# 64 wide attention of a fused transformer kernel: scores two heads at a time, turning two pairs behind, reciprocals of sums by pair

## What is computed

```python
def _L2_xattn_ref(x, context, w_q, w_k, w_v, w_o, b_o):
    HEADS = 16
    DIM_HEAD = 64
    SCALE = DIM_HEAD ** (-0.5)
    q = (x @ w_q).reshape(B, Sq, HEADS, DIM_HEAD).transpose(0, 2, 1, 3)
    k = (context @ w_k).reshape(B, Skv, HEADS, DIM_HEAD).transpose(0, 2, 1, 3)
    v = (context @ w_v).reshape(B, Skv, HEADS, DIM_HEAD).transpose(0, 2, 1, 3)
    sim = jnp.einsum('bhid,bhjd->bhij', q, k) * SCALE
    attn = jax.nn.softmax(sim, axis=-1)
    out = jnp.einsum('bhij,bhjd->bhid', attn, v)
    return out.transpose(0, 2, 1, 3).reshape(B, Sq, INNER) @ w_o + b_o
x = x + jnp.tanh(g_xattn[2]) * _L2_xattn_ref(_layernorm(x), ctx_768, ...)
```

## Time and profile before

| | |
|---|---|
| median of 3 runs | 2455.58 us |
| the profiled execution: its time, its span | 2458.67 us, 2456.9 us |
| PE matmul busy over the span | 1932.6 us (79%) |
| DVE, ACT, POOL busy | 1015.9, 732.9, 999.5 us |
| stage l2x, from its first scores to the last gathered copy | 990.9 to 1573.4 us |
| PE at L1900, L1913, L1928: share of the span on the chain that ended last | 5%, 3%, 3% |

### The profile page before, as it was taken

The page is one execution under the profiler, slowest core; times in us unless marked ns, Lnnn a source line. Parts: engine busy times, 40 slices in busy tenths (PEclk is TensorE's granted clock), DMA queues, the critical chain, the costliest instruction groups (busy, mean ns, idle before and its releaser), DMA issues.

```text
span 2456.9 us, 33526 instructions
## 1 busy us (share of the span) xinstructions
PE 1932.6 (79%) x11738; PEld 1465.6 (60%) x11738; DVE 1015.9 (41%) x2339; ACT 732.9 (30%) x1721; POOL 999.5 (41%) x1044
## 2 busy tenths in 40 slices
PE   3589599727999962898988989769981899647997
PEld 2477466426888852555655656569970666435664
DVE  2434478531222212433334323543223578443773
ACT  1122056302222210332333323312330355312564
POOL 4010443064666643432344323461666676303320
PEclk9799789558999985888988989879995689766999
DMA  4270446114565543000000000012752645004441
GB/s 141 96 259 0 61 75 99 56 65 149 186 200 187 199 149 124 4 3 3 3 0 3 3 3 0 1 54 65 248 165 68 88 67 76 2 0 67 77 72 40
DMA packets 123393, 194.15 MB, mean 79 GB/s; under 512 B 12128, under 2 KB 99168, under 8 KB 122560
## 3 DMA queue, kind: packets, MB, share of 16 engines
q1 hardware_dynamic: 94288, 144.84, 24.6%
q0 software_dynamic: 8480, 26.65, 3.4%
q10 hardware_dynamic: 20496, 20.97, 2.6%
HBM read 109.84 MB, written 43.52 MB: 62 GB/s over the span
## 4 chain that ended last, share of the span: by engine, by line
PE 61%; issue 15%; POOL 9%; DVE 8%; DMA 3%; SPq 2%; ACT 2%; DVEq 0%; POOLq 0%; ACTq 0%
PE bank L2264 8%; PE bank L1774 6%; PE bank L2051 5%; PE bank L1900 5%; PE bank L1775 5%; PE bank L1776 5%; PE bank L1877 5%; PE bank L2085 3%; PE bank L1913 3%; PE bank L1928 3%; POOL arena L853 2%; PE bank L1890 2%; DVE nmf L1133 2%; SPq L582 1%; POOL rows_by_expert L835 1%
## 5 line engine op out<-in xcount | busy, mean ns | idle before, releaser
L1133 DVE TENSOR_REDUCE nmf<-bank 128x2 f32<-128x512 f32 x384 | 257.4, 688 | 144.8 <-PE bank L2051 142.9
L1625 ACT ACTIVATE pT<-bank 128x512 f32<-128x512 f32 x384 | 225.5, 595 | 224.2 <-PE bank L2065 222.7
L1774 PE MATMUL bank<-split,ewl 128*128 128x256 f32 x818 | 245.3, 300 | 9.6 <-DVE split L1361 9.6
L1371 DVE TENSOR_TENSOR arena<-sil,bank 128x256 f32<-128x256 f32 x216 | 91.1, 422 | 358.9 <-ACT sil L1709 358.8
L1776 PE MATMUL bank<-split,ewh 128*128 128x256 f32 x818 | 233.2, 285 | 0.0
L1775 PE MATMUL bank<-split,ewh 128*128 128x256 f32 x818 | 233.1, 285 | 0.0
L2051 PE MATMUL bank<-kpack,qpack 48*128 48x256 f32 (+1 forms) x768 | 199.6, 361 | 33.1 <-DVE nmf L1133 18.9
L889 POOL TENSOR_TENSOR esum<-esum,minus 128x2 f32<-128x2 f32 x128 | 89.2, 697 | 324.4 <-ACT arena L1555 324.2
L1489 ACT ACTIVATE arena<-bank 128x512 f32<-128x512 f32 x162 | 96.7, 597 | 388.4 <-PE bank L2264 158.5
L2264 PE MATMUL bank<-ew,arena 128*128 128x256 f32 (+1 forms) x864 | 210.2, 389 | 2.1 <-issue 2.1
L823 POOL TENSOR_TENSOR ewl<-ew,ewh 128x1536 fp32r<-128x1536 f32 (+1 forms) x71 | 206.9, 2914 | 5.7
(11 more groups left out here) (403 smaller groups left out, 3844.1 us busy)
## 6 DMA issues: line engine op xcount, KB each, us to landing
ew<-in_we SPq DMA_DIRECT2D x46, 768.0 KB, 4.5
rows_by_expert<-mrow ACTq DMA_DIRECT2D x1, 20480.0 KB, 62.8
qpack<-qhl SPq DMA_DIRECT2D x144, 128.0 KB
kpack<-khl SPq DMA_DIRECT2D x144, 128.0 KB
ew<-in_we SPq DMA_DIRECT2D x23, 640.0 KB, 5.5
ew<-in_we SPq DMA_DIRECT2D x25, 512.0 KB, 4.4
arena<-rows_by_expert SPq DMA_DIRECT2D x46, 256.0 KB, 3.8
rows_by_expert<-arena SPq DMA_DIRECT2D x46, 256.0 KB, 4.1
```

Source lines behind the costliest of these rows:

```text
L1133: V.tensor_reduce(nmf[:, c, :, j, r], bank[h % 2][:, :].rearrange("p (t k) -> p t k", t=T), AXX, ALU.max, negate=True).then_inc(m["mx"], 1)
L1625: A(pT16[i % 8][:, :], bank[2 + h % 2][:, :], ACT.Exp, scale=s.qscale).then_inc(m["e"], 1)
L1774: mm(out_, al, bh, start=start, stop=False)
```

## The change

- PE's scores come by pair p (heads 2p and 2p + 1). The four matmuls alternate: queries 0 to 127 of the even head, of the odd head, then queries 128 to 255 of both. The pair waits for the exponentials of head 2p - 2 (its second bank is that head's).
- PE's `heads` goes over pairs: scores of pair p, turn_probs of both heads of pair p - 2, values of pair p - 3. At p = 4 the turning of xn stands between the turns and the values.
- DVE goes over pairs too: both maxima, then both copies of pair p - 2. The statistics of batch n + 1 come behind the copies of p = 2, xn behind those of p = 4. In batch 7 the statistics for the next stage come once per pair.
- POOL takes the sums of a pair to the power -1 in one 128 x 4 operation, then makes the two products. The root comes behind pair 0, that is behind two products in place of one.
- ACT has the same exponentials and gathered copies, by pair.
- prob has 5 buffers in place of 3, and probT 6 in place of 8, in the same room.

```diff
@@ -357,8 +356,8 @@
         qT = q8
         kT = cut(8 * S).rearrange("p (g s) -> p g s", g=8)
         v = cut(T * NH * 64).rearrange("p (t n) -> p t n", t=T)
-        prob = [cut(512) for _ in range(3)]
-        probT = [cut(512) for _ in range(8)]
+        prob = [cut(512) for _ in range(5)]
+        probT = [cut(512) for _ in range(6)]
         oTs = cut(8 * S).rearrange("p (g s) -> p g s", g=8)
         on = [sb(f"on{t}", [P, D]) for t in range(T)]
         xt2 = arena[:, ARENA - DC * S:ARENA].rearrange("p (c s) -> p c s", c=DC)
@@ -883,16 +882,18 @@
                     m = ph[name]
 
                     def normalise(n, ahead):
-                        for h in range(NH):
-                            pool.wait_ge(m["e"], n * NH + h + 1)
-                            nc.gpsimd.tensor_tensor(esum[:, h, :], esum[:, h, :], minus1[:, 0:T], ALU.pow)\
+                        for p in range(PAIRS):
+                            pool.wait_ge(m["e"], n * NH + 2 * p + 2)
+                            sums = esum[:, 2 * p:2 * p + 2, :]
+                            nc.gpsimd.tensor_tensor(sums, sums, minus1[:, :].rearrange("p (h t) -> p h t", t=T), ALU.pow)\
                                 .then_inc(m["psum"], 1)
-                            pool.wait_ge(m["psum"], n * NH + h + 1)
-                            p3 = prob[h % 3].rearrange("p (t k) -> p t k", t=T)
-                            nc.gpsimd.tensor_tensor(p3, p3, esum[:, h, :].rearrange("p (t o) -> p t o", o=1)
-                                                    .broadcast_to([P, T, S]), ALU.mult).then_inc(m["pn"], 1)
-                            if h == 0 and ahead:
+                            pool.wait_ge(m["psum"], n * PAIRS + p + 1)
+                            for h in (2 * p, 2 * p + 1):
+                                p3 = prob[h % 5].rearrange("p (t k) -> p t k", t=T)
+                                nc.gpsimd.tensor_tensor(p3, p3, esum[:, h, :].rearrange("p (t o) -> p t o", o=1)
+                                                        .broadcast_to([P, T, S]), ALU.mult).then_inc(m["pn"], 1)
+                            if p == 0 and ahead:
                                 root(m, n + 2, rstd[:, :], rstd[:, :], mhalf[:, 0:T])
 
                     root(m, 1, rstd[:, :], rstd[:, :], mhalf[:, 0:T])
@@ -1044,27 +1045,30 @@
                         src = bank[s.jobs[j]][:, :].rearrange("p (k s) -> p k s", k=2)
                         ts(qT[:, 2 * j:2 * j + 2, :], src, s.qscale, None, ALU.mult).then_inc(m["qc"], 1)
 
-                def heads(n, ahead, steps_=None):
-                    for h in steps_ or range(LAG, NH + LAG):
-                        if h < NH:
-                            dve.wait_ge(m["s"], n * NH + h + 1)
-                            V.tensor_reduce(nmax[:, h, :], bank[h % 3][:, :].rearrange("p (t k) -> p t k", t=T),
-                                            AXX, ALU.max, negate=True).then_inc(m["mx"], 1)
-                        if h >= LAG:
-                            k = h - LAG
-                            dve.wait_ge(m["pT"], n * NH + k + 1)
-                            if k >= 8:
-                                dve.wait_ge(m["pv"], n * s.groups + (k - 8) // s.per + 1)
-                            V.tensor_copy(probT[k % 8][:, :], bank[3 + k % 2][:, :]).then_inc(m["pTc"], 1)
-                        if h == LAG and ahead:
+                def maximum(n, h):
+                    dve.wait_ge(m["s"], n * NH + h + 1)
+                    V.tensor_reduce(nmax[:, h, :], bank[h % 3][:, :].rearrange("p (t k) -> p t k", t=T),
+                                    AXX, ALU.max, negate=True).then_inc(m["mx"], 1)
+                def turned_weights(n, k):
+                    dve.wait_ge(m["pT"], n * NH + k + 1)
+                    if k >= 6:
+                        dve.wait_ge(m["pv"], n * s.groups + (k - 6) // s.per + 1)
+                    V.tensor_copy(probT[k % 6][:, :], bank[3 + k % 2][:, :]).then_inc(m["pTc"], 1)
+                def heads(n, ahead):
+                    for p in range(1, PAIRS + 2):
+                        for h in (2 * p, 2 * p + 1):
+                            if p < PAIRS:
+                                maximum(n, h)
+                        for h in (2 * p, 2 * p + 1):
+                            if p >= 2:
+                                turned_weights(n, h - 4)
+                        if p == 2 and ahead:
                             statistics(n + 1)
-                        if isinstance(n, int) and n == B - 1 and 0 <= h - 4 < B - 1 and not steps_:
-                            stats_of(h - 4)
-                        if h == FRONT and ahead:
+                        if isinstance(n, int) and n == B - 1 and 2 <= p < 2 + (B - 1):
+                            stats_of(p - 2)
+                        if p == 4 and ahead:
                             front(n + 1)
 
                 def finish(n):
...
                         .then_inc(m["oc"], 1)
 
-                def heads(n, steps_=None):
-                    nf = 0
-                    for h in steps_ or range(LAG, NH + LAG + 2):
-                        if h < NH:
-                            act.wait_ge(m["mx"], n * NH + h + 1)
-                            if h >= 3:
-                                act.wait_ge(m["pT"], n * NH + h - 2)
-                            for t in range(T):
-                                ins = A(prob[h % 3][:, t * S:(t + 1) * S], bank[h % 3][:, t * S:(t + 1) * S], ACT.Exp,
-                                        bias=nmax[:, h, t:t + 1], accum_out=esum[:, h, t:t + 1])
-                            ins.then_inc(m["e"], 1)
-                        if h == FRONT + 1 and not isinstance(n, int):
+                def exponent(n, h):
+                    act.wait_ge(m["mx"], n * NH + h + 1)
+                    if h >= 5:
+                        act.wait_ge(m["pT"], n * NH + h - 4)
+                    for t in range(T):
+                        ins = A(prob[h % 5][:, t * S:(t + 1) * S], bank[h % 3][:, t * S:(t + 1) * S], ACT.Exp,
+                                bias=nmax[:, h, t:t + 1], accum_out=esum[:, h, t:t + 1])
+                    ins.then_inc(m["e"], 1)
+                def heads(n):
...
+                            if p < PAIRS:
+                                exponent(n, h)
+                        if p == 5 and not isinstance(n, int):
                             front(n + 1)
-                        if nf < s.fills and h == min((nf + 1) * 2 * s.per - 1 + LAG + 2, NH + LAG + 1):
-                            gathered(n, nf)
-                            nf += 1
-                    assert steps_ or nf == s.fills
+                        if p >= 5 and p % 2 == 1:
+                            gathered(n, (p - 5) // 2)
 
                 front(0)
                 projected(0)
-                heads(0, range(LAG))
+                for h in range(2):
+                    exponent(0, h)
                 with act.Fori(0, B - 1) as n:
                     heads(n)
                     projected(n + 1)
-                    heads(n + 1, range(LAG))
+                    for h in range(2):
+                        exponent(n + 1, h)
                 heads(B - 1)
 
             def packing(s):
@@ -1891,15 +1899,17 @@
                                      start=c == 0, stop=c == s.kt - 1)
                         ins.then_inc(m["v"], 1)
 
-                def scores(n, h):
-                    if h >= 3:
-                        pe.wait_ge(m["e"], n * NH + h - 2)
-                    gr = h // s.per
-                    r0 = 64 * (h % s.per)
-                    for t in range(T):
-                        ins = mm(bank[h % 3][:, t * S:(t + 1) * S], qT[r0:r0 + 64, gr, t * P:(t + 1) * P],
-                                 kT[r0:r0 + 64, gr, :], start=True, stop=True)
-                    ins.then_inc(m["s"], 1)
+                def scores(n, p):
+                    if p >= 1:
+                        pe.wait_ge(m["e"], n * NH + 2 * p - 1)
+                    for t in range(T):
+                        for j in range(2):
...
@@ -1934,22 +1944,19 @@
                     pe.wait_ge(m["qc"], (n + 1) * s.qjobs)
                     pe.wait_ge(m["kc"], (n + 1) * s.qjobs)
                     pe.wait_ge(m["vc"], (n + 1) * s.vjobs)
-                    for h in range(LAG):
-                        scores(n, h)
+                    scores(n, 0)
 
                 def heads(n, ahead):
-                    gr = 0
-                    for h in range(LAG, NH + LAG + 1):
-                        if h < NH:
-                            scores(n, h)
-                        if h < NH + LAG:
-                            turn_probs(n, h - LAG)
-                        if h == FRONT + 1 and ahead:
+                    for p in range(1, PAIRS + 3):
+                        if p < PAIRS:
+                            scores(n, p)
+                        if 0 <= p - 2 < PAIRS:
+                            turn_probs(n, 2 * p - 4)
```

(53 more changed lines are left out.)

## The result

| | before | changed |
|---|---|---|
| median | 2455.19 us (4 runs, 2451.28 to 2457.07) | 2397.62 us (4 runs, 2389.51 to 2402.51) |
| ratio | | 0.9764, 95% interval 0.9732 to 0.9796 |
| profiled execution, span | 2458.67, 2456.9 us | 2394.44, 2392.6 us |
| stage l2x, first scores to the last finish | 582.59 us | 531.88 us |
| all the rest of the span | 1874.3 us | 1860.7 us |

The median fell by 57.6 us, against 58 predicted. The stage itself fell by 50.7, though; the rest of the span, whose instructions are the same, was 13.6 shorter in this trace. In the changed kernel's second trace, on one of these, the stage is 531.97 and the rest 1895.6. So I compare the length of the stage, and the ratio to the kernel before on the same chip.

What follows compares the result with a forecast made beforehand. PE alone was taken to bound the heads at full clock, POOL's root their start. Batches 1 to 6 give -45.1, batch 0 -5, batch 7 -6, batch 5's projection -2: together -58 from 2455.6, 2398 us, range 2380 to 2430.

Steps and rivals of the forecast that it cites:

- A pair at full clock, 3.15: Heads, PE: scores 1.11, turns 1.03 and values 1.01 make 3.15 us a pair against 4.31.
- The start of the heads: From finish's last issue: a new 3.5 us wait on PE, the wait on the root 5 us later, then one for xn.
- The walk: Step-by-step timing of a looped batch's heads from finish's last issue: 40.7 us against 48.0 with the clock as before.
- the new wait for xn: PE turns xn at 22.3 instead of 20.9, behind DVE's maxima and copies; cost 1.5 us at half clock, 2.3 at full.
- the ring: Score banks: a pair's scores wait for exponentials of the pair before; 2.95 us, under PE's 3.15, so not binding.
- The end of the heads, 9.5: From the last scores through maximum, exponentials, power, products, turn, copy, values and gathered to the projection: 9.5 us.
- The clock: Half clock in the heads expected to end sooner than 17.07 us; 39.8 a batch taken, between 38.8 or 38.4 and 40.7.
- Batches 0 and 7: Heads of the first and last batch: 47.2 to about 42 us (-5), and 38.96 to about 33 (-6).
- batch 5's projection: The short half clock in this projection may go: -2 us.
- rival 1: The score-bank ring or POOL binds the pair instead of PE: 2410 or 2430 us; chance 0.15.
- rival 2: The array's halves don't work side by side inside the heads: about 44.5 us a batch, 2434 us; chance 0.06.
- rival 3: Half clock lasts through all the heads, after new idle spans: a batch about 56 us, about 2495 us; chance 0.05.

Runs made afterwards that it cites:

- the old order with its one wait mended: Kernel before, with POOL taking the root of the next batch behind head 3 instead of head 0: ratio 0.9804, stage 531.23 us.
- all three moves: Changed kernel with root behind pair 1, xn behind copies of heads 2 and 3, scores of heads 2 and 3 inside finish: 2360.51 us, ratio 0.949.

## Why the prediction was right, and where its sum was not

- **A pair at full clock, 3.15.** Measured 3.10. The earlier trace rows carried this, and the run without alternation shows that it was read rightly: 1.07 for a pair in either order.
- **The start of the heads.** The walk from the earlier trace rows had scores 4 and 5 at 4.6, turns until 8.1, turn 2 at 12.9, scores 8 and 9 until 18.9, xn at 22.3. Measured from 1058.28: 4.62, 8.14, 13.01, 18.87, 22.16. "A wait of 3.5 us is new", "The wait on the root isn't removed; it comes 5 us later" and the new wait for xn are all there: 3.49, 3.59, 2.19. Two sums in it are off by less than matters: 2 x 3.04 + 1.91 is 7.99 and not 7.9, and the ring adds up to 2.93 and not 2.95.
- **The end of the heads, 9.5.** From the end of the last scores (1090.86) to 1100.27 it is 9.4.
- **The clock: the term that was mis-sized.** "So I expect it to end sooner ... I take the middle, 39.8". The prediction had one fall, 5.3 us in, which was right (5.07), and one spell of half clock. There were three: the first ended after 3.41, the second began in the wait for the product of head 2 and ended after 6.83, and the third came at the end of the wait for xn (1080.41 to 1083.83). With the clock as before the walk gave 40.7; measured 41.8 to 42.0. The walk to 22.3 was right, and then values of pair 1 and part of the scores behind them ran at half clock: 25.1 instead of 23.8 where these values end. Against the 39.8 that went into the sum it is 2 us a batch, 12 in six. The sum had the wait for xn at its length alone, and 39.8 was only the middle between two cases of one spell. The run that moves xn shows the whole price, 4.0 a batch for a wait of 2.19.
- **Batches 0 and 7.** 40.90 and 30.67, where I had 42 and 33: 3.4 better.
- **The sum.** By terms: batches 1 to 6 took 48.0 to 48.5 and once 43.8, 285.4 together, and now 251.1: -34.3, against -45. Batches 0 and 7 give -6.3 and -8.3, against -5 and -6, and batch 5's projection -1.7, against -2. That is -50.6, the whole of what the stage lost, where I had -58. That the median met 58 to within 1 us is luck: of its 57.6 us some 7 lie, by the first traces, in the rest of the program, whose instructions are the same. In the later traces that part is 1902.7 in the one trace of the kernel before, 1895.6 in the changed kernel's and 1895.2 to 1912.2 in its variants, so several us of either sign there are not the change's. Nor is the stage of the kernel before fixed: by the second traces of both kernels the change gains 54.9 there, 4 more than by the first, most of it in batch 0.
- **The rivals.** The ring and POOL did not bind at full clock (rival 1): from pair to pair PE is busy for 3.10 of 3.10 us, and behind the wait on the root POOL appears only at the end of the heads (0.43 and 0.34). With the halves taken away the kernel lost 86 us in the stage, where rival 2 had 36, because what rival 3 names came with it. Half clock through the heads exists, 37.5 us of it, and there the kernel is 1% longer than the one before (1.0103), the stage 31 us longer than its 586.83. It came only where the side by side work was taken away; in the stage of the changed kernel no spell is over 6.83.
- **What was not seen.** The walk held the gain of the pairs and the price of the start side by side, and I never priced the old order with its one wait mended. It gives the same stage (531.23 against 531.97). The changed order has 38 us less of busy PE than that version, and its three waits and 68 us more at half clock take the place of them. With all three moves, which shorten the waits, the stage is 464.6, 66.6 below the old order with its one mended. How far the old order would come with its other waits mended too was not run; PE is busy for 33.27 us of its heads, which alone is over the 29.77 that the heads take in the version with all three moves.

## What to carry to other kernels

Price a new order from the point where its queue starts, not from its steady state: here the steady pair was shorter by 28%, but two new waits at the start and the old one on the root made the whole no better than the old order with its one wait mended. An operation of the next iteration (root, xn) that is slipped into a queue has to stand where its producer is surely done, behind the work that doesn't need it. And a wait in TensorE's queue can cost more than its length, as a spell at half clock may follow it: one of 2.2 us was worth 4.0 to remove. Last, a gain in the heads of a loop body has to be read batch by batch: the power by pair gave 5.5 us in the stage, and none of it in batches 1 to 6.

## What the runs showed of the hardware

- Matmuls of 64 rows in different halves of the array run side by side without being alternated: two heads' 8 float32 records, four of one half and then four of the other, took 1.07 us, one head's 4 took 1.06. The Trainium skill, TensorE: Matmul & The Clock Gate, Part 3, states that matmuls start and end strictly in program order and that weight loads are pulled ahead of them. In strict order only the last of the first head's matmuls could overlap with the second head's, and the eight records would take near twice 1.06 us; by the records of this run that isn't so for this pattern.
- A wait for work on another engine is often followed by a granted clock of 0.5, for a time that differs: from 3.41 to 37.5 us in these runs. The longest came where all scores used one half of the array, though PE was busy for 34.97 of 37.50 us by its records. What ends such a spell was not tested apart.
- The same wait needn't bring a fall. The wait of 2.19 us for xn was followed by one in batches 1 to 6 of the changed kernel, and not in batch 0. With all three moves, waits of 1.1 and 1.8 us stand at the start of the heads of batches 1 to 6, and the clock fell in batches 2 and 5 alone, for 6.83 us each.
